# Graph attention and graph convolution on one core: the low parts of h and h2 move to VectorE, the layer-2 weights' scaling to GpSimd with two stand-bys, and every engine's list is re-ordered

## The reference

```python
h = jnp.maximum(_layernorm(x), 0.0)
# layer 1: 4 heads, layer 2: 1 head
xl   = (h @ W).reshape(B, N, H, F)
asrc = jnp.einsum('bnhf,hf->bnh', xl, a_src); adst = jnp.einsum('bnhf,hf->bnh', xl, a_dst)
e    = leaky_relu(asrc[:, :, None, :] + adst[:, None, :, :], 0.2)
attn = softmax(where(mask[..., None], e, -1e9), axis=1)     # mask = (adj > 0) | eye
out  = jnp.einsum('bsdh,bshf->bdhf', attn, xl) + bias       # elu between the layers
x = x + gat(h)
h2 = jnp.maximum(_layernorm(x), 0.0)
x = x + h2 + einsum('bni,doi->bno', h2, weights) + take(label_bias, adj).sum(axis=2)
```

## Time and profile before

| | us |
|---|---|
| median of 3 runs | 515.46 (514.21 to 515.85) |
| the profiled execution | 515.12, its span 513.4 |

### The profile page before, as it was taken

How to read it: one execution, slowest core, us unless ns; L and a number is a source line. 1 busy time by engine, 2 the same in 40 slices (tenths; PEclk the granted TensorE clock), 3 DMA queues, 4 the chain that set the end, 5 groups by cost and what they waited for, 6 DMA issues and landing times.

```text
span 513.4 us, 15065 instructions
## 1 busy us (share of the span) xinstructions
PE 484.8 (94%) x3428; PEld 418.7 (82%) x3428; DVE 460.9 (90%) x1821; ACT 439.9 (86%) x1604; POOL 387.2 (75%) x556
## 2 busy tenths in 40 slices
PE   4498999999999999999999999999999999999875
PEld 1377898898888888888888888888888889888754
DVE  7878989999999999999999999999999999998763
ACT  2378999999999999999999999999999999988841
POOL 3266887888888878887887878887887888887641
PEclk9999999999999999999999999999999999999996
DMA  8100111111110111111110111111111111000011
GB/s 224 54 32 3 34 34 52 55 45 43 52 52 21 52 52 52 52 32 52 52 46 27 52 52 52 32 52 52 42 32 51 52 52 52 2 24 23 21 42 42
DMA packets 29149, 23.73 MB, mean 46 GB/s; under 512 B 1976, under 2 KB 28860, under 8 KB 29120
## 3 DMA queue, kind: packets, MB, share of 16 engines
q1 hardware_dynamic: 27328, 21.44, 13.6%
q10 hardware_dynamic: 1792, 1.98, 1.6%
HBM read 14.56 MB, written 8.39 MB: 45 GB/s over the span
## 4 chain that ended last, share of the span: by engine, by line
PE 86%; issue 4%; ACT 3%; DVE 2%; POOL 2%; ACTq 1%; DMA 0%; DVEq 0%; POOLq 0%
PE pA L914 10%; PE pY L926 6%; PE pY L927 6%; PE pY L928 6%; PE pX L888 6%; PE pX L887 6%; PE pX L889 6%; PE pC L951 5%; PE pA L907 5%; PE pH L868 4%; PE pH L959 3%; PE pF L970 3%; PE pF L972 3%; PE pF L971 3%; PE pZ L896 3%
## 5 line engine op out<-in xcount | busy, mean ns | idle before, releaser
L449 ACT ACTIVATE L<-L,nmax 128x128 f32<-128x128 f32 x256 | 101.1, 432 | 0.0
L332 POOL TENSOR_TENSOR h_lo<-h,h_hi 128x512 fp32r<-128x512 f32 x64 | 84.1, 1314 | 20.4 <-ACT h_hi L503 19.8
L355 POOL TENSOR_TENSOR hT_lo<-hT_f,hT_hi 128x256 fp32r<-128x256 f32 x64 | 47.4, 740 | 52.8 <-ACT hT_hi L432 52.7
L926 PE MATMUL pY<-w_hi,h_hi 128*128 128x258 f32 x256 | 76.4, 298 | 1.3 <-POOL h_lo L332 1.2
L927 PE MATMUL pY<-w_lo,h_hi 128*128 128x258 f32 x256 | 72.7, 284 | 0.0
L928 PE MATMUL pY<-w_hi,h_lo 128*128 128x258 f32 x256 | 72.4, 283 | 0.0
L348 POOL TENSOR_TENSOR P<-L,rsum 128x512 f32<-128x512 f32 x64 | 66.5, 1039 | 5.6 <-DVE rsum L741 5.6
L914 PE MATMUL pA<-PT,xl 128*128 128x128 f32 x512 | 67.5, 275 | 0.5 <-ACT PT L457 0.5
L914 PEld LDWEIGHTS pA<-PT,xl 128*128 128x128 f32 x512 | 63.0, 192 | 0.7 <-ACT PT L457 0.7
L735 DVE CUSTOM_DVE_ANT_0 L<-pZ,L 128x128 f32<-128x128 f32 x256 | 58.5, 281 | 1.0 <-ACT L L444 0.9
L449 ACT ACTIVATION_READ_ACCUMULATOR L<-L,nmax 128x1 f32 x256 | 59.1, 231 | 0.0
(11 more groups left out here) (156 smaller groups left out, 1688.5 us busy)
## 6 DMA issues: line engine op xcount, KB each, us to landing
x_all<-in_x SPq DMA_DIRECT2D x32, 256.0 KB, 2.8
out<-x_all SPq DMA_DIRECT2D x32, 256.0 KB, 2.2
adj_all<-in_adj SPq DMA_DIRECT2D x32, 128.0 KB, 2.6
x_all<-in_L_gnn_W ACTq DMA_DIRECT2D x2, 512.0 KB, 5.5
rhs<-lhs SPq DMA_DIRECT2D x64, 6.0 KB
rhs<-lhs SPq DMA_DIRECT2D x64, 1.0 KB
x_all<-in_L_gnn_weights ACTq DMA_DIRECT2D x2, 256.0 KB, 8.3
x_all<-in_L_gnn_att_src ACTq DMA_DIRECT2D x1, 128.0 KB, 6.0
```

The lines of the kernel that those rows point to most:

```text
L332: pool.tensor_tensor(h1_lo[p][:, :, :].rearrange("p a b -> p (a b)"), h1[p][:, :], h1_hi[p][:, :, :].rearrange("p a b -> p (a b)").bitcast ...
L449: last = act.activation(L1[p][:, h, :], L1[p][:, h, :], ACT.Exp, bias=nmax1[p][:, h:h + 1], scale=-1.0, accum_out=sum1[p][:, h:h + 1])
L926: pe.matmul(pY[:, 0:C2], h1_hi[p][:, k, :], w2_hi[:, k, :], start=(k == 0), stop=False)
```

## The change

- ScalarE reads pH once for h and once for h2 (the high part); the plain copies `hT_f` and `h2T_f` are gone. VectorE makes the low parts straight from PSUM in one instruction, max(pH, 0) - high. `transpose_h` therefore waits until `low_h2` has read pH, where it waited for ScalarE's read.
- `normalise2` moves from VectorE (a product with a scalar per row) to GpSimd (a product of two tensors, one broadcast).
- GpSimd gets two steps that only wait: `pause_norm2` until VectorE has finished `layer_norm2` of a graph, and `pause_norm1` until it has finished `layer_norm1`. VectorE gets two steps (`count1`, `count2`) that only wait for semaphores of its own.
- The zero counts are copied by a reduction over one element instead of a copy.
- The attention rows are loaded ahead of W1, and the row of b1 is spread over the partitions by a step of its own.
- The lists of all five engines have a new order and new lags.

```diff
-            pipeline(sp, [(store, 8), (load, -6), (spread_src1, -1), (spread_src2, 2)])
+            pipeline(sp, [(store, 7), (spread_src2, 3), (spread_src1, -1), (load, -6)])
...
-            def low_h(g, p):
-                pool.wait_ge(s_hThi, g + 1)
-                if after(g, 2):
-                    pool.wait_ge(s_xl1, g - 1)
-                pool.tensor_tensor(hT_lo[p][:, :, :], hT_f[p][:, :, :], hT_hi[p][:, :, :].bitcast(F32),
-                                   ALU.subtract).then_inc(s_hTlo, 1)
-
-            def low_h2(g, p):
-                pool.wait_ge(s_h2hi, g + 1)
-                if after(g, 2):
-                    pool.wait_ge(s_fin, g - 1)
-                pool.tensor_tensor(h2T_lo[p][:, :, :], h2T_f[p][:, :, :], h2T_hi[p][:, :, :].bitcast(F32),
-                                   ALU.subtract).then_inc(s_h2lo, 1)
+            def normalise2(g, p):
+                pool.wait_ge(s_rsum2, g + 1)
+                if after(g, 2):
+                    pool.wait_ge(s_P2T, g - 1)
+                pool.tensor_tensor(P2[p][:, :], L2[p][:, :], rsum2[p][:, :].broadcast_to([128, 128]),
+                                   ALU.mult).then_inc(s_P2, 1)
 
...
+            def pause_norm1(g, p):
+                pool.wait_ge(s_hn, g + 1)
+
+            def pause_norm2(g, p):
+                pool.wait_ge(s_h2n, g + 1)
...
-            pipeline(pool, [(add_bias2, 2), (low_h, -2), (inverse_std2, 4), (inverse_std1, -3), (mask_off_diagonal, -2), (low_h2, 5),
-                            (normalise1, 0), (split_h1, 1), (low_w1, -3), (low_w2, 0)])
+            pipeline(pool, [(inverse_std1, -3), (low_w1, -2), (mask_off_diagonal, -2), (add_bias2, 1), (low_w2, -1), (inverse_std2, 4), (normalise1, 0), (normalise2, 3), (pause_norm2, 4), (split_h1, 1), (pause_norm1, -3)])
...
-            act.dma_start(w1_f[:, :, :], W1.rearrange("(k p) n -> p k n", p=128)).then_inc(s_w1dma, 16)
             for j, a in enumerate((att_src1, att_dst1)):
                 act.dma_start(rows_in[:, j, :], a.rearrange("h f -> (h f)").unsqueeze(0)).then_inc(s_rowsdma, 16)
-            act.dma_start(rows_in[:, 2, :], b1.unsqueeze(0)).then_inc(s_rowsdma, 16)
+            act.dma_start(w1_f[:, :, :], W1.rearrange("(k p) n -> p k n", p=128)).then_inc(s_w1dma, 16)
+            act.dma_start(rows_in[:, 2, :], b1.unsqueeze(0)).then_inc(s_b1dma, 16)
...
             def relu_h(g, p):
                 act.wait_ge(s_T0, g + 1)
                 if after(g, 2):
-                    act.wait_ge(s_hTlo, g - 1)
                     act.wait_ge(s_xl1, g - 1)
-                psum = pH[:, 0:D].rearrange("p (k n) -> p k n", k=KD)
-                act.activation(hT_f[p][:, :, :], psum, ACT.Relu)
-                act.activation(hT_hi[p][:, :, :], psum, ACT.Relu).then_inc(s_hThi, 1)
+                act.activation(hT_hi[p][:, :, :], pH[:, 0:D].rearrange("p (k n) -> p k n", k=KD), ACT.Relu).then_inc(s_hThi, 1)
...
             def relu_h2(g, p):
                 act.wait_ge(s_T2, g + 1)
                 if after(g, 2):
-                    act.wait_ge(s_h2lo, g - 1)
                     act.wait_ge(s_fin, g - 1)
-                psum = pH[:, 0:D].rearrange("p (k n) -> p k n", k=KD)
-                act.activation(h2T_f[p][:, :, :], psum, ACT.Relu)
-                act.activation(h2T_hi[p][:, :, :], psum, ACT.Relu).then_inc(s_h2hi, 1)
+                act.activation(h2T_hi[p][:, :, :], pH[:, 0:D].rearrange("p (k n) -> p k n", k=KD), ACT.Relu).then_inc(s_h2hi, 1)
...
-            pipeline(act, [(extra2, 4), (exp1, 1), (exp2, 4), (high_w1, -3), (high_w2, 0), (elu_exp, 2), (score_rows2, 3), (copy_b1, -1),
-                           (score_rows1, -1), (extra1, 0), (high_h1, 2), (no_edges, -5), (copy_PT2, 4), (relu_h2, 5),
-                           (features2, 3), (copy_PT1, 1), (relu_h, -2), (place_label_rows, 3)])
+            pipeline(act, [(high_w1, -4), (copy_b1, -4), (exp1, 1), (relu_h, -1), (elu_exp, 2), (score_rows2, 3), (exp2, 4), (no_edges, -4), (score_rows1, -1), (high_w2, -2), (high_h1, 2), (extra1, 0), (copy_PT2, 4), (features2, 3), (copy_PT1, 1), (place_label_rows, 4), (relu_h2, 5), (extra2, 3)])
...
+            def low_h(g, p):
+                dve.wait_ge(s_hThi, g + 1)
+                if after(g, 2):
+                    dve.wait_ge(s_xl1, g - 1)
+                dve.scalar_tensor_tensor(hT_lo[p][:, :, :], pH[:, 0:D].rearrange("p (k n) -> p k n", k=KD), 0.0,
+                                         hT_hi[p][:, :, :].bitcast(F32), ALU.max, ALU.subtract).then_inc(s_hTlo, 1)
+
+            def low_h2(g, p):
+                dve.wait_ge(s_h2hi, g + 1)
+                if after(g, 2):
+                    dve.wait_ge(s_fin, g - 1)
+                dve.scalar_tensor_tensor(h2T_lo[p][:, :, :], pH[:, 0:D].rearrange("p (k n) -> p k n", k=KD), 0.0,
+                                         h2T_hi[p][:, :, :].bitcast(F32), ALU.max, ALU.subtract).then_inc(s_h2lo, 1)
+
...
+            def count1(g, p):
+                dve.wait_ge(s_lo1, g + 1)
+
+            def count2(g, p):
+                dve.wait_ge(s_ab2, g + 1)
...
-                dve.tensor_copy(ab2[p][:, 1:LO + 2:LO], of_graph(n0_all, g, 1).broadcast_to([128, 2])).then_inc(s_n0col, 1)
+                dve.tensor_reduce(ab2[p][:, 1:LO + 2:LO], of_graph(n0_all, g, 1).broadcast_to([128, 2]).unsqueeze(2), AX.X,
+                                  ALU.max).then_inc(s_n0col, 1)
...
-            def normalise2(g, p):
-                dve.wait_ge(s_rsum2, g + 1)
-                if after(g, 2):
-                    dve.wait_ge(s_P2T, g - 1)
-                dve.tensor_scalar(P2[p][:, :], L2[p][:, :], rsum2[p][:, :], None, ALU.mult).then_inc(s_P2, 1)
...
-            pipeline(dve, [(weigh_w2_dst, 0), (high_scores2, 3), (zero_counts, 3), (take_off_excess, 2), (low_scores2, 3),
-                           (weigh_w1_src, -2), (features1, 1), (layer_norm2, 5), (sum_w3, 1), (recip2, 4), (recip1, 1),
-                           (elu_max, 2), (normalise2, 4), (low_rows1, -1), (release1, -4), (layer_norm1, -2), (leaky1, 0),
-                           (aggregate1, -4), (residual2, 7), (residual1, 4), (weigh_w1_dst, -2),
-                           (largest_labels, 3), (split_w3, 3), (weigh_w2_src, -2), (stats2, 4), (release2, 4),
-                           (label_terms, 2), (stats1, -5), (aggregate2, 4), (leaky2, 3), (largest_of_rows, 3),
-                           (largest_label, 6)])
+            pipeline(dve, [(features1, 1), (sum_w3, 0), (recip1, 1), (low_h, -1), (largest_labels, 6), (largest_of_rows, 6), (weigh_w2_dst, 0), (count1, 0), (count2, 3), (elu_max, 2), (recip2, 4), (stats1, -4), (weigh_w2_src, -1), (weigh_w1_src, -2), (layer_norm2, 5), (release1, -4), (low_rows1, -1), (aggregate1, -4), (residual2, 6), (leaky1, 0), (release2, 4), (layer_norm1, -2), (residual1, 4), (label_terms, 3), (take_off_excess, 1), (split_w3, 0), (low_h2, 5), (stats2, 4), (leaky2, 3), (aggregate2, 4), (high_scores2, 2), (weigh_w1_dst, -2), (zero_counts, 2), (low_scores2, 2), (largest_label, 9)])
...
-            pe.wait_ge(s_rowsdma, 48)
-            for j, spread in enumerate((pA, pZ, pY)):
+            pe.wait_ge(s_rowsdma, 32)
+            for j, spread in enumerate((pA, pZ)):
                 pe.matmul(spread[:, :], one_row[:, :], rows_in[:, j, :], start=True, stop=True).then_inc(s_spread, 1)
...
+            def spread_b1(g, p):
+                if not first(g):
+                    return
+                pe.wait_ge(s_b1dma, 16)
+                pe.matmul(pY[:, :], one_row[:, :], rows_in[:, 2, :], start=True, stop=True).then_inc(s_b1spread, 1)
...
-                    pe.wait_ge(s_h2hi, g - 6)
+                    pe.wait_ge(s_h2lo, g - 6)
...
-                    pe.wait_ge(s_h2hi, g)
+                    pe.wait_ge(s_h2lo, g)
...
-            pipeline(pe, [(transpose_scores2, 3), (score_terms1, -1), (scores1, 0), (project1, 0), (transpose_P2, 4), (transpose_h2, 5),
-                          (transpose_P1, 1), (attend2, 4), (transpose_w3, 2), (transpose_h, -2), (scores2, 3), (project2, 2),
-                          (sum_w2, 0), (attend1, 1), (convolve, 6), (gather_top_label, 5)])
+            pipeline(pe, [(spread_b1, -1), (transpose_P1, 2), (transpose_h2, 6), (attend2, 5), (sum_w2, 1), (scores2, 4), (project2, 3), (transpose_h, -1), (transpose_w3, 0), (attend1, 2), (transpose_scores2, 3), (scores1, 0), (convolve, 6), (score_terms1, -1), (project1, 0), (transpose_P2, 4), (gather_top_label, 8)])
```

More of the change, by code:

```diff
@@ L171, in gat_graphconv_block @@
         hT_hi = two("hT_hi", [128, KD, 128], F32R)
-        hT_f = two("hT_f", [128, KD, 128])
         hT_lo = two("hT_lo", [128, KD, 128], F32R)
```

12 lines of the change are left out of this document (6 added, 6 removed).

## The result

The changed kernel takes 500.25 us, median of 3 runs (499.16 to 501.3), against 515.46: a ratio of 0.971, 95% interval 0.9668 to 0.9752. The forecast was 498.5, its range 493 to 508. The profiled execution took 501.3 us with a span of 499.5.

What follows compares the result with a forecast made beforehand. TensorE was taken to set the slot. Opening 61.0, steady part 399.6 and drain 35.5 sum to a 496.1 us span; 1.7 around it and 0.3 for the median give 498.1, forecast as 498.5, range 493 to 508.

Steps and rivals of the forecast that it cites:

- The steady part: The 57 slots with one graph entering each: from 7.285 to 7.01 us per slot, 399.6 us, 15.6 less.
- the held product: `normalise2` on VectorE, held by GpSimd, makes TensorE's transpose of P2 wait; part of 0.15 us uneven waiting per slot.
- R1: Rival, chance 0.22: VectorE arrives while GpSimd is inside an instruction, layer norms stay long; slots near 7.15, 506 us.
- the first term: Uneven waiting in the steady part, put on the held `normalise2` and layer norm `hn`: 0.15 us per slot would go.
- The pH term: TensorE's `transpose_h` waits in every slot until ScalarE's second read frees pH: 0.13 us per slot would go.
- Point (a): ScalarE loses two plain copies, about 0.4 us each per graph; no direct gain, but pH's single read leaves earlier.
- Point (c): Moved steps stay in time: `transpose_h` comes later, a chain of about 1.6 us fits into some 2.3.
- VectorE's load: VectorE's busy time per slot in the steady part: 6.5 us, or 6.9 if `hn` is still held.
- The stand-bys: GpSimd's two waiting steps cost it idle time only, 0.4 to 0.6 us each per slot.
- The opening: The stretch before the steady part, 61.7 us: earlier loads and moved weight steps give -0.7, from -3 to +3.
- Drain: The stretch after the steady part, 36.5 us: the last graph's chain gets shorter, -1.0, from -3 to +1.5.
- R2: Rival, chance 0.08: stand-bys close a ring, late `split_h1` delays TensorE, then VectorE again; slots of 7.4, 520 us.
- R3: Rival, chance 0.04: low parts in VectorE's queue hold pH as long as before; slots 7.25 to 7.3, about 514 us.

Runs made afterwards that it cites:

- e5_old_scale: The kernel before, in its old order, with only `normalise2` moved to GpSimd (low parts stay on GpSimd, no stand-bys): 507.21 us.
- e2_scale_dve: The changed kernel with `normalise2` put back on VectorE, new order and stand-bys kept: 500.10 us.
- e1_no_standby: The changed kernel without GpSimd's two stand-bys (`pause_norm1`, `pause_norm2`): 499.80 us.
- e5b_old_both: The kernel before, in its old order, with low parts on VectorE and `normalise2` on GpSimd, no stand-bys: 519.59 us.
- e3_low_pool: The changed kernel with the low parts back on GpSimd and ScalarE's double reads of pH, new order and stand-bys kept: 521.12 us.
- a2_after: The changed kernel itself, unedited, run again beside variants of the opening: 499.68 us.
- e8_w2_later: The changed kernel with `low_w2`, GpSimd's split of W2, moved behind `normalise1`: 498.56 us.
- e6_th_back: The changed kernel with `transpose_h` again right behind `attend2`: 574.66 us.
- e9b_sum_free: The changed kernel without stand-bys, with `low_w2` behind `normalise1` and the sums of W2's rows in slot -1: 499.58 us.

## Why the prediction was right

**The steady part.** Forecast 57 x 7.01, -15.6; measured 57 x 7.035, -14.25. Both terms were of the right size: 0.135 per slot for the held product (forecast 0.15; before to e5_old_scale) and 0.115 for pH (forecast 0.13; e5_old_scale to the changed kernel). The second is seen at its place too: the mean distance from `attend2` to its successor fell by 0.11, and its most common value from 0.57 to the 0.44 that the prediction had read in the drain.

**Which edit brings which term** was told less well. Under R1 I wrote that the product "is off VectorE in any case" as if that were needed; e2_scale_dve shows that the new order alone frees it. And the first term took the held `hn` in with the product: e1_no_standby and e5_old_scale both have `hn` held and no uneven slots. In the 7.57 slot of the earlier trace rows no wait of TensorE names `hn`; over the steady part it cost TensorE under 0.01 per slot.

**The pH term is brought by the order.** Point (a) gave the single read of pH as a reason. It is not one: low parts on VectorE in the old order lengthen the hold of pH by 0.14 on the mean (e5b_old_both), and with the double read and the low parts on GpSimd the new order is rid of the wait all the same (e3_low_pool, 0.44 behind `attend2`). Point (c), that `transpose_h` has moved 1.5 us away and the chain of 1.6 fits into 2.3, is the step that carries it: in the slot shown the chain from L965 to the end of L723 is 307.39 - 305.62 = 1.77, of 2.38. What moving the low parts does is to take 1.4 us per slot off GpSimd, which with its stand-bys is over-full in e3_low_pool. Whether that move is needed without the stand-bys is open, and with it whether the order alone would bring the whole gain.

**VectorE's load.** Forecast 6.5 per slot, measured 6.28; GpSimd 4.9 and 4.87; ScalarE 6.0 and 6.14. The prediction took the mean of L780, 0.766, as near its median, which is 0.903; in the steady part alone the mean is 0.818. It also left out that `h2n` was held, by 0.12 on the mean there (0.535 before, 0.415 now). `normalise2` on GpSimd: 0.45 taken, 0.40 measured. The doubling that the Trainium skill gives (GPSIMD Engine Reference, section 4.1) would be 2 x 0.286 = 0.57, an estimate from its factor and L792 of e2_scale_dve; here it is 1.4 times, and the measurement decides.

**The stand-bys** cost idle time only, as said, in the steady part. In the opening no cost of their own is shown. Slot 6 is at 60.69 without them (e1_no_standby) and at 62.85 and 62.04 with them. But slot 1 differs by 0.4 only (28.23 against 28.63 in a2_after), and most of the rest arises between slots 1 and 2, where the clock is low in both profiles of the changed kernel. With `low_w2` moved it is the other way round: 59.17 with them, 61.01 without.

**The opening** was the mis-sized term: -0.7 forecast, +1.16 measured, inside its -3 to +3. I priced the moved steps by their own durations and did not look at what a 2.17 us instruction of GpSimd would meet on VectorE; e8_w2_later shows 1.4 us for that meeting at slot 1, and as much again between slots 1 and 2, where its clock is not low.

**Drain**: -1.0 forecast, -0.8 measured. This agreement is partly luck, as the second execution has 34.6.

**The rivals.** R1's condition (the norms stay long) was made true in e1_no_standby and its price did not come: slots stayed at 7.034, not 7.15. R2's ring did not close: `split_h1` waits for h2n 55 times, 0.4 at most, and TensorE never waits for it in the steady part. R3's condition, pH held as long as before, is what e5b_old_both shows in the old order, and e6_th_back in the new one: the forecast hung on where `transpose_h` stands.

**The sum.** The profiled span is 499.5 where the sum had 496.1: 1.4 of it in the steady part, 1.9 in the opening. The forecast of the median came nearer, 498.5 against 500.25, because the profiled execution is the slowest of the three; that is luck.

## What to carry to other kernels

Moving work between engines and moving an order are not additive: here the low parts in the old order cost 30 us, the new order without them but with the stand-bys costs 6, all together gain 15. An experiment that takes one part out should not leave in another part that the first had made room for, as e3_low_pool leaves the stand-bys. Before crediting a wait that is gone to an edit, find the row in which the bounding engine waits for it; an engine with time to spare may be held for free. In the opening, price a long GpSimd instruction by what VectorE does at the same moment.

## What the runs showed of the hardware

Three things were new to me. First, when a hold ends. In the changed kernel 56 of 64 `h2n` start inside GpSimd's L354, 0.14 to 0.33 us before its end, and take 0.40 to 0.48; in e1_no_standby `hn` starts 0.46 to 0.53 before the end of the mask product 30 times and takes 0.62 to 0.68. A held layer norm of 256 columns ends about 0.15 us behind GpSimd's instruction, also where it started 1.2 us before that end (L707 of the kernel before, 1.35 in all). The tail is not the same for all: the product of 128 columns (L780) ends 0.08 behind GpSimd's instruction, and L597, 1024 columns from two tensors, 1.09 behind it (23.81 against 22.72 in the changed kernel). So a layer norm that starts within 0.25 us of the end loses nothing, unless GpSimd's next instruction follows at once: in the kernel before, 13 of the L780 start 0.01 to 0.03 before the end of L362 and take 1.09 to 1.10, held by L348 behind it, and one `h2n` with 0.12 left takes 0.96. The Trainium skill (SBUF — State Buffer, section "SBUF: two separate sides") has the lock for a whole instruction; the trace agrees but for this tail.

Second, GpSimd's instructions on one or two columns do not hold VectorE: in the kernel before, 11 `h2n` start inside its root of two columns (L326, 0.70 us), with 0.46 to 0.55 of it left, and take 0.40 to 0.41.

Third, time gained in the opening is not kept where the clock answers: TensorE's granted clock fell to 0.50 to 0.57 for some microseconds in the changed kernel (both profiles) and in e9b_sum_free, and not in e1_no_standby or e8_w2_later. The changed kernel and e1_no_standby hardly differ ahead of it: TensorE waits 0.86 and 0.49 in slots 0 and 1 of the one (L861, L882), 0.83 and 0.49 in the other. What decides it stays open.
